# Macaron block on one core: the feed-forward's orders of VectorE, ScalarE and GpSimd over a pair of tiles are rewritten

## The reference

```python
x = x + 0.5 * ffn(layernorm(x)); x = x + causal_attention(layernorm(x)); x = x + 0.5 * ffn(layernorm(x))

def fp4_quant_dequant(x):            # blocks of 16 along the last axis
    scale = max(max(abs(block)) / 6, 1e-12)
    return GRID[searchsorted(MID, abs(block / scale))] * sign(block) * scale
def fp4_linear(x, w): return einsum('bsk,nk->bsn', fp4_quant_dequant(x), fp4_quant_dequant(w))
def ffn(x): return fp4_linear(silu(fp4_linear(x, w_gate)) * fp4_linear(x, w_up), w_down)   # 256 -> 704 -> 256
```

## Time and profile before

| | |
|---|---|
| median of 3 runs | 1241.42 us (1240.62 to 1241.96) |
| the profiled execution | 1241.77 us, of which the span from first to last instruction is 1239.6 |
| PE busy | 1156.6 us, 93% |
| DVE busy | 1006.2 us, 81% |
| ACT busy | 789.2 us, 64% |
| POOL busy | 554.1 us, 45% |
| chain that ended last | PE 74%, DVE 13%, ACT 5%, issue 4%, DMA 2% |
| first stage, steady part | about 76 to 360 us |
| second stage, steady part | about 906 to 1220 us |

### The profile page before, as it was taken

The page is one execution under the profiler, slowest core; times in us unless marked ns, Lnnn a source line. Parts: engine busy times, 40 slices in busy tenths (PEclk is TensorE's granted clock), DMA queues, the critical chain, the costliest instruction groups (busy, mean ns, idle before and its releaser), DMA issues.

```text
span 1239.6 us, 24264 instructions
## 1 busy us (share of the span) xinstructions
PE 1156.6 (93%) x7673; PEld 751.8 (61%) x7673; DVE 1006.2 (81%) x2809; ACT 789.2 (64%) x1599; POOL 554.1 (45%) x531
## 2 busy tenths in 40 slices
PE   1689999999998689999999999999999999999997
PEld 1256666666665456676676667566566666666664
DVE  7899999999999576556656654664689999999996
ACT  4768888888864345434544543565578888887863
POOL 2444554455444244435443453445244455554441
PEclk9889999999999899999999999999999999999999
DMA  6955544544444356555664646457255555555565
GB/s 219 242 98 88 95 86 93 95 93 84 88 85 84 80 113 113 102 116 100 117 117 97 116 94 131 84 90 122 49 85 119 121 117 109 115 110 111 121 122 113
DMA packets 462739, 134.33 MB, mean 108 GB/s; under 512 B 441296, under 2 KB 461904, under 8 KB 462672
## 3 DMA queue, kind: packets, MB, share of 16 engines
q1 hardware_dynamic: 454928, 125.62, 52.0%
q10 hardware_dynamic: 7744, 7.86, 2.0%
HBM read 11.34 MB, written 8.39 MB: 16 GB/s over the span
## 4 chain that ended last, share of the span: by engine, by line
PE 74%; DVE 13%; ACT 5%; issue 4%; DMA 2%; SPq 1%; POOL 1%; DVEq 0%; ACTq 0%; POOLq 0%
PE ps L1481 33%; PE ps L1442 17%; PE ps L1528 12%; PE ps L1516 9%; DVE arena L1138 2%; PE ps L1501 2%; PE ps L1494 2%; ACT arena L797 2%; DVE arena L1125 1%; DMA arena<-arena 1%; ACT arena L789 1%; SPq L418 1%; DVE arena L1101 1%; DVE arena L969 1%; DVE arena L973 1%
## 5 line engine op out<-in xcount | busy, mean ns | idle before, releaser
L1481 PE MATMUL ps<-wguT,arena 128*128 128x512 f16 (+1 forms) x2304 | 479.9, 363 | 6.8 <-DMA arena<-arena 6.7
L1481 PEld LDWEIGHTS ps<-wguT,arena 128*128 128x128 f16 x2304 | 225.9, 98 | 228.3 <-issue 9.6
L549 POOL TENSOR_TENSOR arena<-arena 128x704 f32<-128x704 f32 x128 | 193.4, 1511 | 253.8 <-DVE arena L982 253.8
L1442 PE MATMUL ps<-wdT,arena 128*128 128x256 f16 x2176 | 263.6, 276 | 25.0 <-DMA arena<-arena 16.7
L1442 PEld LDWEIGHTS ps<-wdT,arena 128*128 128x128 f16 x2176 | 214.3, 99 | 68.0 <-DMA arena<-arena 15.4
L576 POOL TENSOR_TENSOR arena<-arena 128x128 f16<-128x128 f32 (+7 forms) x64 | 143.9, 2248 | 229.7 <-ACT arena L797 127.4
L806 ACT ACTIVATE arena<-ps,arena,cst 128x128 f16<-128x128 f32 (+7 forms) x64 | 80.5, 1258 | 192.5 <-DVE arena L1143 188.5
L1528 PE MATMUL ps<-arena 128*128 128x256 f16 x1632 | 190.5, 274 | 9.9 <-DVE x_sb L1154 9.8
L1516 PE MATMUL ps<-arena 128*128 128x512 f16 (+3 forms) x960 | 186.9, 347 | 2.6 <-ACT arena L797 2.6
L1528 PEld LDWEIGHTS ps<-arena 128*128 128x128 f16 x1632 | 159.0, 98 | 38.2 <-DVE x_sb L1154 13.5
L727 ACT ACTIVATE arena<-arena 128x704 int16<-128x704 f32 x128 | 100.8, 787 | 112.8 <-POOL arena L549 112.8
(11 more groups left out here) (128 smaller groups left out, 1405.5 us busy)
## 6 DMA issues: line engine op xcount, KB each, us to landing
out_dram<-x_sb SPq DMA_DIRECT2D x32, 256.0 KB, 2.7
x_sb<-in_L_attn_x_dram ACTq DMA_DIRECT2D x3, 2048.0 KB, 8.8
arena<-arena SPq DMA_TRANSPOSE x384, 3.5
arena<-arena SPq DMA_DIRECT2D x8, 256.0 KB, 2.9
arena<-arena SPq DMA_DIRECT2D x4, 512.0 KB, 3.0
x_sb<-in_L_attn_x_dram ACTq DMA_DIRECT2D x1, 1536.0 KB, 7.5
arena<-in_L_ffn_w_down_dram SPq DMA_DIRECT2D x1, 704.0 KB, 7.7
arena<-in_L_ffn_w_gate_dram SPq DMA_DIRECT2D x1, 640.0 KB, 4.6
```

What stands on the lines that cost most here:

```text
L549: g.tensor_tensor(hy[u].rearrange("p (j b) -> p b j", j=BL), h[u].rearrange("p (b j) -> p b j", j=BL), hri[u].unsqueeze(2).to_broadcast([P ...
L1442: i = nc.tensor.matmul(ps_dn[w % 2], hT[w][:, c * P:(c + 1) * P], wdT[:, k, :], start=(s == 0), stop=(s == len(DOWN_STEPS) - 1))
L1481: i = nc.tensor.matmul(psf[:, 1536 * u + lo:1536 * u + hi], xv[:, u, xl, kt, :], wguT[:, wl, lo // P:hi // P, kt, :], start=(s == 0), stop ...
```

## The change

It moves instructions of the three pair functions, adds none and removes none. `pool_pair` inside the loops: `pool_x_var` goes ahead of the first product of h, and `pool_x_root` between the two products (in the pairs written out, where gp is a number, the variance stays behind the first product). `act_pair`: the squares go behind the second silu, h's factor `act_h_fc` right behind that silu, and x of gp + 3 ahead of the rounding for gp + 2. `dve_pair`: `dve_x_q` and `dve_h_pow` go behind `dve_h(a + 2)`, `dve_h_sp` behind them, the maxima of h(a + 2) and the second `dve_res` (with `dve_last_add(TB - 1)`) come after `dve_h_sd`; `dve_h_q` of tile a - 1 and `dve_h_rin(a + 1)` come ahead of `dve_x_g` and `dve_h_max`.

```diff
--- before.py
+++ after.py
@@ -591,16 +591,20 @@
 
 
         def pool_pair(gp, odd, x3=True, x4=True, z1=False):
+            static = isinstance(gp, int)
+            if x4 and not static:
+                pool_x_var(gp + 4, odd)
             pool_h_y(2 * gp, 0)
             if x4:
-                pool_x_var(gp + 4, odd)
+                if static:
+                    pool_x_var(gp + 4, odd)
+                pool_x_root(gp + 4)
             if z1:
                 pool_z_lo(1)
             pool_h_y(2 * gp + 1, 1)
             if x3:
                 pool_x_y(gp + 3)
             if x4:
-                pool_x_root(gp + 4)
                 pool_x_shift(gp + 4, odd)
 
         @block.gpsimd
@@ -752,21 +756,21 @@
                 act_x_mean(gp + 4, p + 4, odd)
             if start != 0:
                 act_h_c(a - 1, 1)
-            if x4:
-                act_x_squares(gp + 4, p + 4, odd)
             act_silu(a + 1, 1)
+            if start != 0:
+                act_h_fc(gp - 1, 1 - odd)
             if z1:
                 act_z_hi(1)
                 act_load_table(ACT.Exp)
+            if x4:
+                act_x_squares(gp + 4, p + 4, odd)
+            if x3:
+                act_x_z(gp + 3, p + 3)
             if x2:
                 act_x_n(gp + 2)
                 act_x_c(gp + 2)
-            if x3:
-                act_x_z(gp + 3, p + 3)
             act_h_n(a, 0)
             act_h_c(a, 0)
-            if start != 0:
-                act_h_fc(gp - 1, 1 - odd)
 
         def act_z_hi(g):
             nc.scalar.wait_ge(z_z, g + 1)
@@ -1056,42 +1060,44 @@
                 dve_last_add(TB - 2)
             dve_h_amax(a + 1, 1)
             if x2:
-                dve_x_g(gp + 2)
+                dve_x_sl(gp + 2)
             dve_h_s(a + 1, 1)
-            if x2:
-                dve_x_sl(gp + 2)
-            dve_h_max(gp)
             if start != 0:
                 dve_h_q(gp - 1, 1, quad(qd, 2 * odd - 3))
+            dve_h_rin(a + 1, 1)
+            if x2:
+                dve_x_g(gp + 2)
+            if x3:
+                dve_x_amax(gp + 3)
+            dve_h_max(gp)
+            if not end:
+                dve_h(a + 2, 0)
+            if x3:
+                dve_x_s(gp + 3)
+            dve_h_pow(gp)
+            dve_h_g(a, 0)
+            dve_h_inv(gp)
             if x2:
                 dve_x_q(gp + 2, 0, (qd + odd, 1 - odd))
                 dve_x_q(gp + 2, 1)
-            dve_h_pow(gp)
-            dve_h_rin(a + 1, 1)
-            dve_h_inv(gp)
-            if x3:
-                dve_x_amax(gp + 3)
             dve_h_sp(gp)
-            if not end:
-                dve_h(a + 2, 0)
-            dve_h_g(a, 0)
-            dve_h_sd(gp)
-            if x3:
-                dve_x_s(gp + 3)
-            dve_h_sh(gp)
             if x3:
                 dve_x_rin(gp + 3)
-            dve_h_sl(gp)
+            dve_h_sd(gp)
+            if not end:
+                dve_h_amax(a + 2, 0)
             if start is None:
                 dve_res(gp - 2, odd, 1, p * 2 - 3)
             if adds:
                 dve_last_add(TB - 1)
-            if not end:
-                dve_h_amax(a + 2, 0)
-                dve_h_g(a + 1, 1)
-                dve_h_s(a + 2, 0)
+            dve_h_sh(gp)
             if x3:
                 dve_x_sd(gp + 3)
+            if not end:
+                dve_h_g(a + 1, 1)
+            dve_h_sl(gp)
+            if not end:
+                dve_h_s(a + 2, 0)
             dve_h_q(gp, 0, quad(qd, 2 * odd - 2))
```

## The result

The changed kernel takes 1246.20 us (median of 6 runs, 1245.20 to 1247.53); the kernel before took 1241.10 beside it (6 runs, 1239.54 to 1241.96). The ratio is 1.0037, with an interval of 1.0028 to 1.0047, so +3.5 to +5.8 us; by the medians +5.1. The forecast was +6.4, or 1247.8. The profiled execution took 1247.53 us with a span of 1245.4, 5.8 more than before.

A forecast was written before the change was run, and what follows sets the result against it. PE was taken to set the steady period, 10.84 us per pair. The terms 2.3 + 0.6 + 1.5 + 1.6 + 0.4 gave +6.4 us on 1241.77: 1248.2, or 1247.8 as median; range 1243 to 1252, chance 0.68.

The forecast's parts named there:

- Steady part, 0: Steady pairs: DVE gains 0.8 us per pair, but PE does not wait for DVE, so zero for 54 pairs.
- The margin of x's transpose: Steady pairs: time between x's transpose landing and the gate products needing it falls from 3.9 to 1.2 us.
- the first rival: Steady pairs: the 1.2 us margins fail and PE waits 0.2 us per pair, +11 us, about 1259; chance 0.08.
- First start, +2.3: First stage's start: x of pair 2 quantized behind h of tile 2 delays SP's queue; +2.3 us, bounds +1.5 and +3.3.
- First stage's end, +0.6: First stage's end: shorter loop against later second `dve_res`, and tile 61's quantization chain later; +0.6 us, bounds -2.0 and +2.0.
- the waits for the second `dve_res` 0.5 us longer: First stage's end, last four pairs: PE's waits for each pair's second `dve_res` grow by 0.5 us.
- about the same: First stage's end: vanishing `dve_res` waits and 1.6 us of half clock save 5.7 us; about 1241.5, chance 0.14.
- The two opposing effects: First stage's end: loop up to 0.8 us shorter per pair, against second `dve_res` 2.6 us behind h instead of 1.1.
- Second start, +1.5 and +1.6: Second stage's start: later last addition makes PE wait +1.5 us; half clock behind it adds +1.6, bounds 0 and +2.7.
- the row nearest to 4.5 us of idle: Second stage's start: idle of 4.5 us is nearest to 4.72, which half clock followed, so half clock was taken.
- The end, +0.4: Kernel's end: last two quantizations and transposes come some 0.45 us later behind POOL's product; +0.4 us, bounds 0 and +0.8.
- The rule: Steady pairs: `pool_x_root` reading SBUF would hold DVE's two-input instructions, up to 0.6 us more per pair; sum unchanged.

The follow-up runs named there:

- experiment 4: Kernel before with h's small scaling alone moved behind h of tile a + 2: 1241.91 us, ratio 0.9993.
- the second profile: Changed kernel run again, unedited, with a profile of 1245.64 us: median 1247.18 us, ratio 1.0039.
- 6: Changed kernel with the down weights' six transposes ahead of the transpose of x of pair 2 in SP's queue: 1248.75 us, ratio 1.0061.
- 7: Changed kernel with the down weights' transposes ahead of x of pair 2's, and the last addition ahead of h of tile 68: 1243.17 us, ratio 1.0016.
- 8: Kernel before with h's scaling behind h(a + 2), down weights' transposes ahead of x of pair 2's, last addition ahead of h of tile 68: 1240.29 us, ratio 0.9985.
- experiment 1: Changed kernel with the attention's last addition directly behind h of tile 68: 1244.26 us, ratio 1.0015.
- 3: Changed kernel with x of pair 2 quantized ahead of h of tile 2, and the last addition directly behind h of tile 68: 1241.46 us, ratio 0.9996.
- 11: Changed kernel with x of pair 2 quantized ahead of h of tile 2, and the last addition ahead of h of tile 68: 1239.80 us, ratio 0.9988.
- 2: Changed kernel with x of pair 2 alone quantized ahead of h of tile 2: 1245.18 us, ratio 1.0027.
- 10: Changed kernel's DVE order with the ACT and POOL orders of before: 1247.00 us, ratio 1.0040.

## Why the prediction was right

**Steady part, 0.** Right, by experiment 4 above all: 0.8 us of blocking per pair goes, DVE waits instead, and the period stays 10.84. The margin of x's transpose was put at 1.2 us; it is issued at 206.41, lands 3.1 us later by its median, and its gate products start at 211.06: 1.55. The waits of PE in each pair, the first rival, did not come.

**First start, +2.3.** The mechanism was right, and its times to 0.3 us: h at 54.8 and the transpose at 57.0 were forecast, 54.78 and 56.91 measured in the second profile; the six transposes take 7.94 us start to start (8.0 forecast); the first down product was put at 70.2 and came at 69.95. The two profiles give +1.3 and +3.2 once the clock is full again. Two things were left out. A stretch at half clock ahead of it, at about 52 us, can delay h of tile 2 by 1.76 us (56.54 against 54.78). That stretch is no doing of the change: it stands in 10 of the 14 profiles, of both kernels' orders, and is missing in the one of the kernel before, in the second one of the changed kernel and in those of 4 and 6. And the half clock after the wait costs less than before when the wait is longer, since more of it falls on idle time: from the first to the second down product 8.00 us passed before, 7.37 and 7.21 now. The first adds, the second subtracts, and +2.3 stands in the middle by luck as much as by working.

**First stage's end, +0.6.** It came out at -0.7 and -0.5. The step that failed is "the waits for the second `dve_res` 0.5 us longer": the sizes are near (0.41, 1.08 and 2.58 before; 0.75, 0.70 and 2.81 now), but the half clock that stood behind the third one, which the sum kept without saying so, is gone. From 384.00 to 387.40 it took PE 3.40 us to come to its next product, from 387.41 to 389.27 1.86: that is 1.54 us. Without it the step is +0.9. The rival "about the same" named this 1.6 us and asked for the waits to vanish as well; they did not. Whether the change took the half clock away stays open: it is missing in seven of the nine profiles with DVE's new order and stands in those of 6 and 7, and of the five with the order of before only that of 8 lacks it. The two opposing effects that the step weighed were both real: with the scaling alone moved (4) the three waits are none, none and 2.73 us, so the shorter loop does reach PE, and the rest of the new order gives that back.

**Second start, +1.5 and +1.6.** Measured +1.40 by the wait (4.38 against 2.98) and +1.68 and +1.67 by the clock in the two profiles. It is the largest part and the surest, and choosing the half clock by the row nearest to 4.5 us of idle was the right call. In experiments 1, 3, 7 and 11 the half clock does not come, and the wait is 1.92 us or none.

**The end, +0.4.** +0.2: the waits there are 1.01, 1.89, 2.61 and 0.59 us; the chain is as forecast and its delay half as large.

**The rule.** L1034, with two SBUF inputs, starts at 201.49 inside `pool_x_root` (201.33, 0.69 us) and takes 0.89 us; its median over the run is 0.893. So the root holds nothing that counts. The Trainium skill, SBUF — State Buffer, section "Who interferes with whom", would have the whole of a GpSimd instruction that reads SBUF hold it; for this small product the trace disagrees, and the measurement decides. For the 1.5 us products on 128 x 704 the trace agrees: L1008 beside none takes 0.24 us, and L1004 beside one took 1.05.

**The sum.** The forecast for the profiled execution was +6.4; it gave +5.8 and, the second time, +3.9. The ratios give +3.5 to +5.8. The forecast is right in sign and in its two causes, and by the medians 1.3 us too large, about the 1.5 us of the half clock that vanished at the first stage's end. That the sum is so near is in part luck, since the first stage's end came out with the other sign. The bounds given for the parts add up to +1.0 and +10.3; the range said +2.5 to +10.4, and its lower end was so narrower than the parts allowed.

## What to carry to other kernels

An engine at 99.8% that holds nobody up is worth nothing to relieve where that is so, here in the steady part: look for a wait of the engine that sets the period before paying for a new order. Where one order of instructions is used for the steady part and for the starts of stages, price the starts by themselves: they are where a moved step has no cover, and one wait that grows from 3 to 4.4 us can also cost as much again in clock. Here what paid was the reverse of the change, to put the one instruction PE waits for ahead of the one that waits for PE.

## What the runs showed of the hardware

- The same kernel, in two profiles, had PE's clock full at 51.90 to 55.25 (after 2.55 us of idle) and at half (after 3.66 us); before it was full after 2.97. At the first stage's end a wait of 2.58 us was followed by half clock and one of 2.81 was not; at the second start 2.98 and 1.92 were not, and 4.38 was, in each of the five profiles that have it (the two of the changed kernel and those of 2, 6 and 10). Ahead of the place at 52 us, a wait of 1.74 us (1) and one of 2.79 (3) were followed by half clock, and waits of 3.19 (6) and 3.28 (4) were not; at the first stage's end the same wait of 2.8 us was in 6 and 7 and was not in 1, 2, 3, 10, 11 and the two of the changed kernel. Up to 3.7 us the length of the wait alone does not tell. What does was not tried.
- A stretch of 3.4 us at half clock costs 1.5 to 1.7 us where PE has work all through it.
- Small transposing DMAs issued beside the bulk loads of the input (DMA share 1.17 in the window 50 to 66) took 8.6 us to land and 2.4 to issue, against 2.8 and 1.28 later. Issued from 47.1 us on, the six held SP's queue for 14.4 us; issued from 60.0 on, for 7.9.
- A gain read in one profile came out smaller in the median of 11 runs (4.1 and 2.7 us for experiment 1, though the interval holds both). Single executions of one kernel differ by 1.6 to 5.1 us, and the stretches at half clock come and go between them. That this is all of the difference is my reading and was not shown.
